# Dissolving the weight preparation of a four-layer gated transformer kernel into its first turn

## What is computed

```python
x = x + tanh(g_xattn[0]) * L0_xattn(layernorm(x), ctx, Wq, bq, Wk, bk)   # softmax(QK'/sqrt(512)) @ ctx
x = x + tanh(g_ffn[0])   * L0_ffn(layernorm(x))       # base W + top-2 of 8 LoRA experts
x = x + tanh(g_xattn[1]) * L1_xattn(layernorm(x), ctx)  # windowed attention over the feature axis
x = x + tanh(g_ffn[1])   * L1_ffn(layernorm(x))       # base W + routed experts
x = x + tanh(g_xattn[2]) * L2_xattn(layernorm(x), ctx)  # low-rank attention, 16 heads
x = x + tanh(g_ffn[2])   * L2_ffn(layernorm(x))       # sign(weight), routed channel scales
x = x + tanh(g_xattn[3]) * L3_xattn(layernorm(x), ctx, ctx, pos, mask)  # 32 heads, 8 K/V heads, rope
x = x + tanh(g_ffn[3])   * L3_ffn(layernorm(x))
```

## Time and profile before

| | before |
|---|---|
| median of 3 runs | 2186.48 us |
| the profiled execution | 2186.74 us |
| its span in the trace | 2184.9 us |
| PE busy | 1860.1 us (85%) |
| DVE busy | 1671.9 us (77%) |
| ACT busy | 557.4 us (26%) |
| POOL busy | 599.5 us (27%) |
| early layers' first transpose | 87.18 us after the start |

### The profile page before, as it was taken

How to read it: one execution, slowest core, us unless ns; L and a number is a source line. 1 busy time by engine, 2 the same in 40 slices (tenths; PEclk the granted TensorE clock), 3 DMA queues, 4 the chain that set the end, 5 groups by cost and what they waited for, 6 DMA issues and landing times. The chain is left out here.

```text
span 2184.9 us, 37129 instructions
## 1 busy us (share of the span) xinstructions
PE 1860.1 (85%) x14832; PEld 1034.9 (47%) x14832; DVE 1671.9 (77%) x2989; ACT 557.4 (26%) x1290; POOL 599.5 (27%) x717
## 2 busy tenths in 40 slices
PE   4388788887788888988855899999999999999876
PEld 3344455444554355533632355555555555555432
DVE  3379766798658966699644788888888888888875
ACT  3121223222342123222224122222222222222221
POOL 0220114102140023300224443434343434343210
PEclk7689978999899987999967999999999999999987
DMA  7436501473033720436013211111111111110100
GB/s 231 154 103 191 152 2 39 132 204 111 1 103 115 204 63 1 137 116 174 1 43 127 78 49 49 49 49 49 49 50 51 52 51 51 49 30 20 40 25 35
DMA packets 134266, 176.47 MB, mean 81 GB/s; under 512 B 46416, under 2 KB 73200, under 8 KB 133968
## 3 DMA queue, kind: packets, MB, share of 16 engines
q1 hardware_dynamic: 134096, 174.10, 26.5%
HBM read 131.98 MB, written 42.08 MB: 80 GB/s over the span
## 5 line engine op out<-in xcount | busy, mean ns | idle before, releaser
L1156 POOL TENSOR_TENSOR early_vare<-early_mv,w_eps 128x1 f32<-128x1 f32 x96 | 30.1, 313 | 779.0 <-DVE early_mv L1222 764.9
L379 PE MATMUL la_ps<-w_xTh,w_wqh 128*128 128x512 bf16 x512 | 198.4, 388 | 15.4 <-DVE la_rot L2271 10.3
L2210 POOL TENSOR_TENSOR la_q<-la_straight,la_rot 128x512 f32<-128x512 f32 x128 | 163.1, 1274 | 164.7 <-DVE la_rot L2271 164.7
L379 PE MATMUL la_ps<-w_woh,la_oTh 128*128 128x512 bf16 x512 | 199.2, 389 | 0.0
L380 PE MATMUL la_ps<-w_wol,la_oTh 128*128 128x512 bf16 x512 | 198.8, 388 | 0.0
L750 PE MATMUL early_ps<-early_products,w_heads 128*32 128x512 f32 x1024 | 146.0, 698 | 61.0 <-DVE early_products L1373 34.9
L381 PE MATMUL la_ps<-w_woh,la_oTl 128*128 128x512 bf16 x512 | 197.8, 386 | 0.0
L380 PE MATMUL la_ps<-w_xTl,w_wqh 128*128 128x512 bf16 x512 | 196.7, 384 | 0.0
L381 PE MATMUL la_ps<-w_xTh,w_wql 128*128 128x512 bf16 x512 | 196.6, 384 | 0.0
L2223 POOL TENSOR_TENSOR la_p<-la_s,la_rec 128x256 f32<-128x256 f32 x128 | 89.6, 700 | 322.4 <-DVE la_rec L2292 322.4
L2161 ACT ACTIVATE la_oTh<-la_ps 128x256 bf16<-128x256 f32 x256 | 84.2, 381 | 303.1 <-PE la_ps L2073 303.1
(11 more groups left out here) (345 smaller groups left out, 4535.2 us busy)
## 6 DMA issues: line engine op xcount, KB each, us to landing
early_vR<-scr_v SPq DMA_DIRECT2D x128, 257.0 KB, 5.2
early_wkv<-wkv SPq DMA_DIRECT2D x32, 512.0 KB, 4.6
la_v<-v SPq DMA_DIRECT2D x64, 256.0 KB, 3.9
k<-early_ctxt SPq DMA_DIRECT2D x32, 256.0 KB, 3.7
v<-early_ctxt SPq DMA_DIRECT2D x64, 128.0 KB, 3.1
scr_p<-early_weights SPq DMA_DIRECT2D x16, 512.0 KB, 3.1
early_pR<-scr_p SPq DMA_DIRECT2D x32, 256.0 KB, 3.4
w_raw_q<-in_Wq SPq DMA_DIRECT2D x8, 1024.0 KB, 6.9
```

Source lines behind the costliest of these rows:

```text
L379: pe.matmul(out, lh[c], rh[c], start=(first and c == 0), stop=False)
L2210: rope_sum.send(pool.tensor_tensor(dst, straight[:, slot, :], rot[:, slot, :], ALU.add))
```

## The change

`prepare_weights` and its stage are gone. Its steps are methods of a class `Preparation`, which `early_layers` calls at chosen places of each engine's program; its tiles lie in SBUF that the early layers use later (xTf and what follows; the K/V staging lies in `pR`, the split K/V groups in `wkv`, the mask of negative weights in `xq`).

- SP loads Wq, Wk and the biases, then x, then R0 and W0, then cT, the small tables, the context and the other weights. After product s is complete (the staging overlaps earlier tiles) it loads the first two K/V groups (2 x 256 KB each).
- The 20 DMAs of weights that need no work are issued by ACT (`load_direct`) after the tanh of the gates.
- R0 and W0 are split before the product's halves; R1, W1, Wqd, Wkv and R3 by ACT after the first xTh, and by DVE after each of the four `aT` of turn 0 (`first_turn`), followed by the two instructions for the sign of W2.
- The K/V weights are split in eight groups: high by ACT, low now by POOL, each group written to `wkv3` (512 KB) and the next but one loaded into its buffer.
- The memset of `comb2` moves from the start into each turn of POOL, with a semaphore for DVE.

```diff
+    def load_kv(self, sp, g):
+        if g >= 2:
+            sp.wait_ge(self.kv_low, g - 1)
+        for i, name in enumerate(("Wk3", "Wv3")):
+            src = self.io[name].rearrange("(c p) n -> p c n", p=P)[:, :, g * HD:(g + 1) * HD]
+            sp.dma_start(self.staging[:, g % 2, i, :].rearrange("p (c n) -> p c n", c=C), src)\
+              .then_inc(self.kv_in[g % 2], 16)
+    def keep_kv(self, sp, g):
+        sp.wait_ge(self.kv_low, g + 1)
+        sp.dma_start(self.io["wkv3"][g], self.kv_split[:, g % 2, :, :, :, :].rearrange("p i l c n -> p (i l c n)"))\
+          .then_inc(self.kv_kept[g % 2], 16)
+    def split_kv_high(self, act, *gs):
+        for g in gs:
+            act.wait_ge(self.kv_in[g % 2], 32 * (g // 2 + 1))
+            if g >= 2:
+                self.wait_kv_kept(act, g - 2)
+            act.activation(self.kv_split[:, g % 2, :, 0, :, :].rearrange("p i c n -> p i (c n)"),
+                           self.staging[:, g % 2, :, :], ACT.Copy).then_inc(self.kv_high, 1)
+    def split_kv_low(self, pool, *gs):
+        for g in gs:
+            pool.wait_ge(self.kv_high, g + 1)
+            pool.tensor_tensor(...
+                               ALU.subtract).then_inc(self.kv_low, 1)
...
 # SP, in early_layers
+            def first_keys_values(*gs):
+                for g in gs:
+                    prep.keep_kv(sp, g)
+                    if g + 2 < KV:
+                        prep.load_kv(sp, g + 2)
             def attention1(turn):
-                load_kv_weights(turn, 0)
-                load_kv_weights(turn, 1)
+                if turn == 0:
+                    first_keys_values(0, 1, 2, 3)
+                else:
+                    load_kv_weights(turn, 0)
+                    load_kv_weights(turn, 1)
                 for j in range(QUAD):
                     banks.wait_drained(sp, turn, "v1", j)
                     v_written[j % 2].send(sp.dma_start(scr_v[j], vp[:, j % 2, :]))
                     if j == 1:
                         for k in range(2):
                             load_values(sp, turn, k)
+                if turn == 0:
+                    first_keys_values(4, 5, 6, 7)
+                    for g in range(2):
+                        prep.wait_kv_kept(sp, KV - 2 + g)
+                        load_kv_weights(turn, g)
...
 # POOL, turn 0
+                if turn == 0:
+                    prep.split_kv_low(pool, 0, 1, 2, 3)
+                    pool.wait_ge(prep.biased, 1)
                 rstd_of(turn, 1)
                 add_bias(turn, 0, 1)
+                if turn == 0:
+                    prep.split_kv_low(pool, 4, 5, 6, 7)
                 rstd_of(turn, 2)
...
 # DVE, after each aT of turn 0
+            def first_turn(j):
+                if j == 0:
+                    prep.low(dve, "R1")
+                elif j == 1:
+                    prep.low(dve, "W1")
+                elif j == 2:
+                    prep.low(dve, "Wqd", "Wkv", "R3")
+                else:
+                    prep.below_zero(dve)
+                    prep.signs(dve)
```

More of the change, by code:

```diff
@@ L388, in early_layers @@
 def early_layers(nc, io, w):
+    opening = [(("M", m), m) for m in range(C)] + [(("r",), 4), (("c",), 5), (("s",), 6)]
     plan = []
@@ L481, in early_layers @@
             aTl = sb("aTl", [P, QUAD, C, P], HALF, stack=first)
+        with ExitStack() as unsplit:
+            prep = Preparation(nc, io, w, unsplit, xq, pR, wkv)
         xTf, osb = sb("xTf", [P, QUAD, C, P]), sb("osb", [P, QUAD, D])
@@ L492, in early_layers @@
         scr_p = nc.dram_tensor("scr_p", (QUAD, P, WIN * TP), F32).ap()
-        banks = Banks(nc, ctx, w, "early", plan)
+        banks = Banks(nc, ctx, w, "early", plan, opening)
         x_loaded = [signal(f"x_loaded{j}", 1, 16) for j in range(QUAD)]
@@ L622, in store @@
                     stored.send(sp.dma_start(io["x_mid"][bass.ts(turn * QUAD + j, P), :], xq[:, j, :]))
-            sp.wait_ge(pads, 5)
+            prep.load_product(sp)
             for j in range(QUAD):
                 load_x(j, j)
+            prep.load_raw(sp, "R0", "W0")
+            for j in range(QUAD):
                 load_cT(j, j)
+            prep.load_rest(sp)
+            for j in range(QUAD):
                 load_ctx(j, j)
+            prep.load_raw(sp, "R1", "W1", "Wqd", "Wkv", "R3", "W2")
+            prep.keep_positions(sp)
+            banks.wait_filled(sp, 0, "s")
+            sp.wait_ge(prep.pos_kept, 16)
+            prep.load_kv(sp, 0)
+            prep.load_kv(sp, 1)
             for turn in range(TURNS - 1):
@@ L959, in body @@
                 ffn2(turn, more)
+            prep.product(pe, banks)
+            prep.wait_constants(pe)
             ahead(0)
+            prep.wait_direct(pe)
             for turn in range(TURNS - 1):
@@ L1188, in body @@
                 rstd_of(turn, 5)
+                comb2_cleared.send(pool.memset(comb2[:, :, :], 0.0))
                 if more:
@@ L1294, in body @@
                                 "proj0", j)
+                    if turn == 0:
+                        first_turn(j)
                 def row_term(j):
@@ L1528, in body @@
                 st.close()
-            dve.wait_ge(pads, 5)
+            prep.zero(dve)
             body(0, True, "statistics")
             body(0, True, "normalised")
+            prep.low(dve, "R0", "W0")
+            prep.positions(dve)
+            prep.product_low(dve, banks)
             body(0, True, "lows")
+            prep.small_tables(dve)
+            prep.wait_direct(dve)
+            dve.wait_ge(pads, 4)
             for turn in range(TURNS - 1):
@@ L2453, in build @@
             with stage(nc, w):
-                prepare_weights(nc, io, w)
-            with stage(nc, w):
                 early_layers(nc, io, w)
```

396 lines of the change are left out of this document (218 added, 178 removed).

## The result

| | before | changed |
|---|---|---|
| median | 2187.7 us (4 runs, 2184.53 to 2192.15) | **2161.85 us** (4 runs, 2160.32 to 2166.48) |
| ratio | | 0.9887 (95%: 0.9861 to 0.9914) |
| the profiled execution | 2186.74 us | 2166.48 us |
| its span | 2184.9 us | 2164.7 us |

The account below looks back on a forecast made before the run. A serial 51.2 us hole on TensorE in the opening was taken as the bound. Removing it, -51.2, and +20 given back in turn 0 make -31.2 us: from 2186.74 to 2155.5 us, range 2142 to 2169 us.

Parts of the forecast that it names:

- The opening: TensorE's empty stretch from 35.98 to 87.18 us goes, as transposes of x follow the bias products: -51.2 us.
- Step 1: Turn 0, DVE: 3.5 us of sign work behind the fourth aT adds nothing, since ACT is later than that.
- step 2: Turn 0: ACT splits groups 0 and 1, POOL's low half takes 2.3 us, group 2's split precedes prT: +5 us.
- Steps 3 and 4: Turn 0: POOL's first root behind group 3's low half puts the last xn at +9; groups 4 and 5 leave +9.
- Step 5: Turn 0: group 6's loads queue behind SP's shifted loads, landing in 8 us; hsT behind its split: total +19.
- Step 6: Turn 0: idle TensorE's clock falls, about 1 us; first keys' product at +20; nothing later makes up or adds delay.
- the chain: The turn 0 delays as derived, giving back 20 us of the opening's gain: 2149 to 2161 us, chance 0.60.
- the queue doesn't hold: Rival: group 6's loads are not held back or waits overlap better; turn 0 gives back 10 to 12 us: 2146.5 us, 0.19.
- The opening slips: Rival: ACT's 20 issues take 22 us or weights arrive late, delaying aT_high 3 to 5 us: about 2165 us, 0.15.
- Slower than before: Rival: six reloaded K/V groups each make a full round trip with ACT waiting: +29 us, 2215 us, chance 0.04.
- the wait ahead of hsT: Sign: ACT's split of group 6 waits for a DMA, some 8 us or more, just ahead of hsT.
- the split of group 2 ahead of prT: Sign: on ACT this split waits for a DMA, some 4 to 5 us, just ahead of prT.

Follow-up runs that it names:

- early_signs: The changed kernel with W2 loaded behind W0 and its two sign instructions run on DVE in the opening, not behind the fourth aT: 2156.86 us.
- late_shifts: The changed kernel with turn 0's sixteen shifted loads of values issued behind all K/V groups and the read-back: 2151.28 us.
- half_late: The changed kernel with eight of turn 0's sixteen shifted value loads ahead of the later K/V loads and eight behind them and the read-back: 2151.9 us.
- all_late: The changed kernel with K/V steps placed anew, signs in the opening and all sixteen shifted loads behind the read-back: 2136.37 us.

## Why the prediction came out right, and which terms were off

**The opening** is as worked out. The forecast was 51.2 us from a hole on TensorE, 51.4 was measured, and ACT's DMA issues, foreseen at 11.3 us, ended at 20.84 us and delayed nothing. A stretch in which the engine that bounds has nothing at all, and whose work for it (here the loads and the layer norm of x) can be done before, can be booked in full. In other executions the same opening starts its transposes up to 3.3 us later; that was in no term.

**Step 1 failed** (sign work of 3.5 us adds nothing, as ACT is later anyway), and with it the low half of **step 2** (2.3 us each, done at 107.5 us). Both are 3.1 us short: prT moved by 8.1 us, not 5. The prediction laid two delays side by side and took the larger. By DVE alone that held: the last exponential ended at 62.37 us, and ACT then still waited 1.38 us for group 2. But the two meet at POOL. DVE's sign instruction waits for POOL's aTl, and POOL's first low half then waits for the sign: the earlier trace rows gave 1.16 us for a subtraction whose successors took 2.48, 1.58 and 1.40. Most of the 3.1 us can be named: 0.6 for a later fourth aT (16.0 us behind the transposes, 15.4 before), 0.24 for the last aTl, 2.0 for the low half. With the signs gone the step gives its +5 (early_signs: 5.0, to within 1 us).

**Steps 3 and 4** came out at +13.4 for the last xn (83.43 us, 47.6 behind the transposes, against 34.2), where 9 was given: 3.1 are step 2's. The rest is pace: the four prT took 8.0 us where 7.2 was given, and from POOL's first root to the last xn 7.7 us went by where 6.8 was given. That POOL's root stands behind the low half of group 3 was in the step, rightly.

**Step 5** had the right place and nearly the right price. The loads of group 6 took 8.2 and 9.3 us to land, where 8 was assumed from the earlier trace rows; ACT waited 13.53 us where at least 8 were foreseen, since it had come to that point early and the loads late. HsT moved by 24.4 us instead of 19, but step 5's own share is 24.4 - 13.4 = 11.0, against 10 predicted. Against the timetable the write of group 4 was issued some 2.5 us late (93.66 us, 145.0 on the clock of before, for 142 to 143), and from it to hsT passed some 2.5 us more than worked out. late_shifts, which takes the queue away, gets 11.0 to 11.9 us back. That confirms the mechanism; half_late shows that its price is not linear.

**Step 6** was right in its own +1 (25.5 - 24.4 = 1.1), and the clock did fall: TensorE stood idle for 8.27 us ahead of the matmuls on hsT, and the granted clock was 0.50 in 100 to 108 us and 0.62 in 108 to 110, where before it was 1.00 in all of 128 to 138. That nothing makes up for a delay holds as far as the times can tell: in the other kernels the median gains 0.9 to 4.2 us more than the product does, and in the changed kernel run again 8.0 us more.

The sum thus was -51.2 + 20 where -51.4 + 25.5 was found, 5.3 us too hopeful; the other 1.0 us is the median before, which a fourth run raised to 2187.7. The median of 2161.85 us is 6.3 us above the forecast, just outside the 2149 to 2161 that the chain had for itself, and inside the whole range. Of the rivals, "the queue doesn't hold" is refuted by the 13.53 us. "The opening slips" named 2165 us, nearer than the forecast, but not by its mechanism: in the profile ACT's issues and the loads held nothing up. A later start by up to 3.3 us does occur, with the clock of the bias products. Slower than before didn't occur: even the sum of all waits gave back half of the gain. That it could all be kept is shown by all_late.

Of the signs named, the transposes right behind the bias products, the wait ahead of hsT and the split of group 2 ahead of prT are there. The wait ahead of prT was 1.38 us, not 4 to 5, since ACT came to it late, the exponentials having waited for the signs on DVE. POOL's first root came at 75.77 us, not 72, and the product at 119.55, not 114. Whether a later turn changes its length can't be said to better than 3 to 4 us: from the first product of one turn to that of the next it is 264.4, 257.8 and 264.5 us before, 262.5, 261.1 and 263.0 in the first profile of the changed kernel, and 260.0, 257.7 and 264.4 in the second.

The rule of the Trainium skill weighed there (GPSIMD Engine Reference, Specifications: shared SBUF interfaces with VectorE, contention with DVE instructions of two SBUF inputs) was right in kind: this trace has a subtraction of 1.16 us take 2.48 beside such a DVE instruction. I was wrong to book nothing because DVE "waits or reads PSUM": POOL met instructions that the change itself added. The 10% that I read from the additions of xq was the wrong size too, as the last section shows.

## What to carry to other kernels

When setup work is dissolved into gaps, first ask of each inserted instruction what stands behind it in order on its engine, and whether that needs it: all but 0.7 of the 25.5 us came back when splits, signs and shifted loads no longer stood in front of prT, the roots and hsT, with the same work done. Two inserted delays on different engines may be merged by taking the larger only if the instructions on them don't hold each other up. And a queue must be costed by when its turn comes: here the first eight loads, which fit into its idle time, cost 1.6 us at the product, and the next eight 10.3.

## What the runs showed of the hardware

**DVE and POOL take turns at instructions with two SBUF inputs.** In the timelines of the changed kernel above, W1's low half runs on DVE from 46.38 to 48.66 us at its full pace, and POOL's aTl, started at 47.21, takes 2.48 us: 1.45 until DVE is done, and 1.03. The sign on DVE starts at 53.66 and takes 3.12 us instead of the 2.29 of the earlier trace rows: POOL's aTl ends at 54.63, 0.97 later. POOL's low half, started at 54.60, takes about 4.1 instead of 2.12: DVE ends at 56.78, 2.18 later. R3's low half on DVE took 1.40 us here and 0.43 before; POOL's aTl ran until 51.59, 1.10 us into it. So the price fits the rest of the other engine's instruction, in both directions, and not a percentage. DVE's aT at 48.58, with one input in PSUM, took 0.68 us beside POOL's aTl and 0.69 before. Early_signs takes the sign instructions away, and POOL's two low halves fall from 6.25 to 4.21 us and its last aTl from 1.40 to 1.16. These 0.24 us lie where DVE's other instruction of the sign work, with one input, was still running (until 53.62), so the price may not be confined to two inputs. That one engine waits for the other's whole instruction is my reading of four pairs; no run moved one instruction alone.

**The opening has two paces.** M's product took 16.15 us in one profile and 16.87 in the other of the same program, and the one-column matmuls of r and c 3.63 and 5.21 us against 4.31 and 6.96. The granted clock fell from its 2.4 to its 1.2 GHz level about 2 us earlier in the second, by the windows above, and TensorE worked without a gap in both. Two of the nine profiles of changed kernels have the quicker opening, and so has the one of before. Why the clock falls at different moments stays open, and so does how often the kernel before has the slower opening; up to 3.3 us of any difference between single profiles here may be that.
